# Router logits of a one-core attention and mixture-of-experts kernel: from transposes and a product on TensorE to products and row sums on VectorE

## The reference

```python
x = layernorm(x + attention(x))      # 16 heads of 16, rotated q and k, softmax over 2048 keys, then @ out_w + out_b
n = layer_norm(x, g1, be1)
y = x + n + (n @ mix_w + mix_b)
n2 = layer_norm(y, g2, be2)
probs = softmax(n2 @ router_w)       # router_w is 256 x 8: eight logits per token
topw, topi = top_k(probs, 2)         # each token goes to two of eight experts
out = y + sum over the two of topw * (silu(n2 @ w1[e] + b1[e]) @ w2[e] + b2[e])   # 256 -> 1024 -> 256
x = layernorm(out)
```

## Time and profile before

| | before |
|---|---|
| median of 3 runs | 1770.38 us |
| the profiled execution | 1769.97 us |
| its span, first to last instruction | 1768.3 us |
| mean granted TensorE clock | 0.966 of full speed |
| TensorE busy | 1646.8 us (93%) |
| ScalarE busy | 1234.6 us (70%) |
| VectorE busy | 534.5 us (30%) |
| GpSimd busy | 491.3 us (28%) |

### The profile page before, as it was taken

How to read it: one execution, slowest core, us unless ns; L and a number is a source line. 1 busy time by engine, 2 the same in 40 slices (tenths; PEclk the granted TensorE clock), 3 DMA queues, 4 the chain that set the end, 5 groups by cost and what they waited for, 6 DMA issues and landing times.

```text
span 1768.3 us, 46251 instructions
## 1 busy us (share of the span) xinstructions
PE 1646.8 (93%) x17948; PEld 934.9 (53%) x17949; DVE 534.5 (30%) x1421; ACT 1234.6 (70%) x1851; POOL 491.3 (28%) x512
## 2 busy tenths in 40 slices
PE   5986999998999999999999999998999999999991
PEld 3642333333333333333333333337899999999991
DVE  3441122633623623623623624634420000000004
ACT  2436899998997997997997997993344444444441
POOL 4750000121121121121121121123445444444441
PEclk9997999999999998999999999999999999999996
DMA  3567410011101153321101101165567766666645
GB/s 114 191 160 110 76 29 23 23 38 42 40 24 38 46 89 74 79 68 38 36 28 38 36 27 39 36 224 177 157 174 215 202 186 190 186 178 178 178 126 198
DMA packets 108822, 181.69 MB, mean 103 GB/s; under 512 B 14041, under 2 KB 80665, under 8 KB 108473
## 3 DMA queue, kind: packets, MB, share of 16 engines
q1 hardware_dynamic: 95346, 161.40, 31.4%
q0 software_dynamic: 13296, 17.77, 5.7%
HBM read 134.59 MB, written 40.18 MB: 99 GB/s over the span
## 4 chain that ended last, share of the span: by engine, by line
PE 77%; issue 4%; ACT 4%; another core or an unknown queue 3%; DVE 1%; DMA 1%; POOL 0%; SPq 0%; POOLq 0%; ACTq 0%; DVEq 0%
PE at_s L1241 23%; PE at_po L1253 22%; PE at_s L1364 14%; PE at_s L1377 13%; ACT place L1154 4%; PE at_small L1269 3%; PE at_small L1262 1%; PE at_po L1353 1%; DMA rows_out<-place,at_v 1%; DVE cb_ln_stats L578 1%; DVE place L1593 0%; POOL place L1097 0%; DMA place<-rows_out 0%; POOL place L1102 0%
## 5 line engine op out<-in xcount | busy, mean ns | idle before, releaser
L1154 ACT ACTIVATE place<-at_s 128x1024 f32<-128x1024 f32 x1024 | 957.9, 1142 | 92.3 <-PE at_s L1241 51.7
L1241 PE MATMUL at_s<-place 99*32 99x512 bf16 x8192 | 590.5, 388 | 35.1 <-ACT place L1154 24.9
L1253 PE MATMUL at_po<-place,at_v 128*32 128x512 f32 x4096 | 555.5, 602 | 9.4 <-issue 9.1
L1241 PEld LDWEIGHTS at_s<-place 99*32 99x32 bf16 x8192 | 202.7, 96 | 518.0 <-issue 250.2
L1364 PEld LDWEIGHTS at_s<-place 128*128 128x128 f32 x2272 | 265.7, 193 | 4.2 <-issue 0.8
L1364 PE MATMUL at_s<-place 128*128 128x128 f32 x2272 | 266.7, 276 | 0.0
L1171 ACT ACTIVATE place<-at_s,b_turned 128x128 f32<-128x128 f32 x568 | 161.8, 368 | 141.4 <-PE at_s L1364 139.5
L1377 PE MATMUL at_s<-place 128*128 x1136 | 256.9, 379 | 0.4 <-issue 0.4
L1377 PEld LDWEIGHTS at_s<-place 128*128 128x128 f32 x1136 | 210.4, 190 | 26.4 <-issue 0.7
L1253 PEld LDWEIGHTS at_po<-place,at_v 128*32 128x32 f32 x4096 | 132.6, 112 | 121.3 <-issue 23.1
L1016 POOL COPY at_v<-place 128x1024 f32<-128x1024 f32 x32 | 33.2, 1041 | 442.3 <-PE at_po L1253 431.7
(11 more groups left out here) (201 smaller groups left out, 971.7 us busy)
## 6 DMA issues: line engine op xcount, KB each, us to landing
place<-in_w SPq DMA_DIRECT2D x79, 1024.0 KB, 9.1
place<-k_parts SPq DMA_DIRECT2D x48, 256.0 KB, 9.3
place<-q_parts SPq DMA_DIRECT2D x192, 64.0 KB
at_v<-rows_in SPq DMA_DIRECT2D x71, 129.0 KB
x_in<-in_x SPq DMA_DIRECT2D x9, 512.0 KB, 4.8
q_parts<-qk_lower SPq DMA_DIRECT2D x16, 256.0 KB, 2.3
k_parts<-qk_lower SPq DMA_DIRECT2D x16, 256.0 KB, 2.5
at_heads_T<-at_o SPq DMA_DIRECT2D x128, 32.0 KB, 1.9
```

Source lines behind the costliest of these rows:

```text
L1154: nc.scalar.activation(probs[:, slot(n), :], p_s[n % BUFFERS][:, :], ACT.Exp).then_inc(exp_done, 1)
L1241: last = nc.tensor.matmul(p_s[n % BUFFERS][j:j + 32, s * 512:(s + 1) * 512], k_rows[0:ROWS_M, quad(q).start + h, kt * P + j:kt * P + j + 3 ...
L1253: last = nc.tensor.matmul(p_o[32 * h:32 * h + 32, :], v_one[q % 2][:, h, kt, :], probs[:, slot(q * NG + g), s * 512:(s + 1) * 512], start= ...
```

## The change

The router's logits are no longer computed by TensorE. `router_w` is loaded spread over all 128 partitions (each partition holds all 256 x 8 weights, 8 KB, by a broadcast load of 1 MB in place of one of 8 KB). For each of the four 128-token tiles of a group and each half of the experts VectorE multiplies the normalised row (256 columns, repeated four times) with the weights of four experts (read with a step of 8 elements, 32 bytes) into `weighted` (128 x 1024), and sums rows to four logits: 8 multiplications and 8 sums per group, each followed by a wait for its own completion. TensorE loses the second transposes and the router product, so a group has 7 jobs on `small`, not 10. The division is split off `copy_out` into `divide` and is placed later than the copy at three places; in unit 1 it stands between the ready signal of the first norm and the copy of the first transposes. The second `layer_norm`'s statistics now stand ahead of `copy_out(i + 1, 0)`, its application behind. TensorE's steps move: first transposes 48, 52 to 38, 40; mix product 56 to 62 to 44 to 50; counting 118 to 100; ScalarE's logit exponential 104 to 88. To make room, `den`, `passed` and the final norm's scratch now share memory with `turned`. In the last group's tail the points 17 to 19 go; the others keep their points.

```diff
 def layer_norm(dve, steps, out, inp, w):
     norm_scale(dve, steps, inp, w)
+    norm_apply(dve, steps, out, inp, w)
...
-    JOBS = 10
+    JOBS = 7
-    NORM_AT = {48: 0, 52: 1}
-    MIX_AT = {56: (0, 0), 58: (0, 2), 60: (1, 0), 62: (1, 2)}
-    SENT_AT = {80: 0, 84: 1}
-    ROUTER_AT = {88: 0, 90: 4}
-    COUNT_AT = 118
+    NORM_AT = {38: 0, 40: 1}
+    MIX_AT = {44: (0, 0), 46: (0, 2), 48: (1, 0), 50: (1, 2)}
+    COUNT_AT = 100
...
-        den = m.sb("at_den", [P, 512], F32)
-        router_w = m.sb("rt_router_w", [P, KC, E], F32)
+        router_w = m.sb("rt_router_w", [P, D, E], F32)
+        den = turned[:, 0, :]
...
-        STEPS = 3 * LN_STEPS + 19
+        STEPS = 3 * LN_STEPS + 19 + 4 * GT
-        TAIL_AT = {2: (14, 16), 3: (18, 20), 9: (48,), 10: (52,), 11: (56, 58), 12: (60, 62),
-                   17: (80,), 18: (84,), 19: (88, 90), 26: (118,)}
+        TAIL_AT = {2: (14, 16), 3: (18, 20), 9: (38,), 10: (40,), 11: (44, 46), 12: (48, 50),
+                   26: (100,)}
...
-                for dst, src in ((out_w, "out_w"), (mix_w, "mix_w"), (router_w, "router_w")):
+                for dst, src in ((out_w, "out_w"), (mix_w, "mix_w")):
                     sp.dma_start(dst[:, :, :], dram[src].rearrange("(s p) n -> p s n", p=P)).then_inc(loaded_w, 16)
+                sp.dma_start(router_w[:, :, :].rearrange("p d e -> p (d e)"),
+                             dram["router_w"].rearrange("d e -> (d e)").partition_broadcast(P)).then_inc(loaded_w, 16)
...
-                        if routed and n == 104:
+                        if routed and n == 88:
                             router(i - 1)
...
                     v.tensor_copy(o_sb[q % 2][:, :], p_o[:, :]).then_inc(o_copied, 1)
+
+                def divide(i, q):
+                    unit = i * UNITS + q
                     dve.wait_ge(o_copied, unit + 2)
...
                     layer_norm(v, steps, x1, x1, w)
+                    norm_scale(v, steps, x1, w)
                     if beside:
                         copy_out(i + 1, 0)
-                    layer_norm(v, steps, norm1, x1, w)
+                    norm_apply(v, steps, norm1, x1, w)
...
                                     ).then_inc(norm1_ready, 1)
-                    if not beside:
+                    if beside:
+                        divide(i + 1, 0)
+                    else:
...
                     dve.sem_inc(x2_ready, 1)
-                    if beside:
-                        copy_out(i + 1, 1)
-                    else:
+                    if not beside:
...
-                    turned_half(0)
-                    turned_half(1)
-                    job.arrived()
-                    logits = small[:, 0:GT * E].rearrange("p (a e) -> p a e", a=GT)
+                    dve.wait_ge(norm2_ready, i + 1)
+                    weighted = turned[:, :, :].rearrange("p k n -> p (k n)").rearrange("p (e d) -> p e d", e=E // 2)
+                    for a in range(GT):
+                        for some in (slice(0, E // 2), slice(E // 2, E)):
+                            steps.then(v.tensor_tensor(weighted, sent_rows[:, 0, a, 0:D].unsqueeze(1)
+                                                       .broadcast_to([P, E // 2, D]),
+                                                       router_w[:, :, some].rearrange("p d e -> p e d"), ALU.mult))
+                            steps.then(v.tensor_reduce(logit[:, a, some], weighted, AX.X, ALU.add))
+                        if a == 0 and beside:
+                            copy_out(i + 1, 1)
...
                     dve.sem_inc(shifted, 1)
-                    dve.sem_inc(small_read, 1)
                     if beside:
-                        copy_out(i + 1, 2)
+                        divide(i + 1, 1)
...
+                    if beside:
+                        copy_out(i + 1, 2)
                     job.arrived()
                     counts = small[:, 0:2 * GT * E].rearrange("p (n a e) -> p n a e", n=2, a=GT)
...
                     v.tensor_copy(pos[:, :, :], pos_f[:, :, :]).then_inc(placed, 1)
+                    if beside:
+                        divide(i + 1, 2)
```

More of the change, by code:

```diff
@@ L602, in layer_norm, with norm_apply @@
     norm_scale(dve, steps, inp, w)
+    norm_apply(dve, steps, out, inp, w)
+def norm_apply(dve, steps, out, inp, w):
     for a in range(GT):
@@ L764, in attend_route_experts @@
         final = room[:, at_quad:at_quad + NT * D].rearrange("p (a n) -> p a n", a=NT)
-        w_final = norm_scratch(m, "cb_ln", NT)
+        place_final = turned[:, 0, :]
+        w_final = {"stats": place_final[:, 0:NT * 6].rearrange("p (a n) -> p a n", n=6),
+                   "bits": place_final[:, NT * 6:NT * 7].bitcast(I32)}
+        w_final.update({n: place_final[:, NT * (7 + k):NT * (8 + k)]
+                        for k, n in enumerate(("var", "apart", "mean2", "rstd", "shift", "half", "t"))})
         loaded_sum = [m.sem(f"cb_loaded{g}") for g in range(PIECES)]
@@ L1308, in route @@
                         return product(mix_w, turned, (2 * half, 2 * half + 1), D, job, (first, first + 1))
-                    elif at in SENT_AT:
-                        pe.wait_ge(norm2_ready, i + 1)
-                        turn(sent_rows[:, 0, :, 0:D], SENT_AT[at], job)
-                    elif at in ROUTER_AT:
-                        first = ROUTER_AT[at]
-                        return product(router_w, turned, range(GT), E, job, range(first, first + 4))
                     elif at == COUNT_AT:
@@ L1565, in _ @@
                     copy_out(0, q)
+                    divide(0, q)
                 dve.wait_ge(loaded_w, 16 * 9)
@@ L1570, in _ @@
                     copy_out(i - 1, UNITS - 1)
+                    divide(i - 1, UNITS - 1)
                     route(i - 1, steps, job, True)
@@ L1575, in _ @@
                 copy_out(LAST - 1, UNITS - 1)
+                divide(LAST - 1, UNITS - 1)
                 making = Chain(dve, made)
@@ L1581, in _ @@
                 copy_out(LAST, UNITS - 1)
+                divide(LAST, UNITS - 1)
                 route(LAST, steps, job, False)
```

7 lines of the change are left out of this document (4 added, 3 removed).

## The result

The changed kernel takes 1857.97 us (median of four runs, 1852.97 to 1866.86) against 1771.52: a ratio of 1.0493, 95% interval 1.0472 to 1.0514. It is **slower by some 87 us**, where the prediction said 32 and a range up to 62. The direction was right, the size was not. All ratios leave out an execution that took over 1.5% longer than the fastest of its kernel; this concerns one of e5.

The account below looks back on a forecast made before the run. TensorE (93%) looks like the limit, but in the attention ScalarE's 32 exponentials a unit (29.4 us) are the floor. From 1770.38 us, −2.7 + 23 + 12.6 − 3 + 2 = +32 gives 1802; range 1744 to 1832.

Parts of the forecast that it names:

- main forecast: Whole kernel: the hole stays with the scatter and VectorE's lateness makes TensorE wait; +32 us, 1802 us, chance 0.47.
- hole: Units 3 and 0: ScalarE idle beside eight indirect DMAs, TensorE's clock at its lower level; together 52 us before.
- unit 1's transposes: First norm's second transposes, step 40: TensorE waits 2.7 us for VectorE's copy behind the division; with +0.6, seven times, +23.
- unit 1's copy: VectorE's p_o copy at unit 1's end, behind the second norm and first products: at about T + 39.7, done T + 40.4.
- The hole's term: Scatter moved to mid-unit 3: bounds −3 (49 of 52 us stay) or −52; −3 us taken.
- a lighter TensorE: Router work removed from TensorE: 0.4 us a group in unit 2, counted there; −2.7 us in the tail.
- I take 1.23, by the casts.: Router's strided multiplication on VectorE: 1.23 us each, between bounds 1.23 and 2.28; a tile of tokens 5.0.
- that rival: Router multiplications: strided reads slow, 2.3 us each, +5 us a group, 1837 us; chance 0.13.
- unit 0's copy: VectorE's p_o copy ending unit 0 (old time T), behind second norm's statistics: 1.8 us late, TensorE waits 1.05, +0.6.
- the step of unit 2: Head of unit 2: TensorE waits 2.2 us for unit 1's copy; unit 31.6 against 29.8, seven times, +12.6.
- Rival 1: Units 3 and 0: the hole goes once the scatter stands mid-unit; 1753 us, 1740 to 1765, chance 0.30.
- Rival 3: Units 1 and 2: VectorE's lateness absorbed by exponentials in hand; 1766 us, 1760 to 1772, chance 0.10.

Follow-up runs that it names:

- e5: Changed kernel with GpSimd waiting for each of the eight indirect DMAs to land: 1818.86 us, ratio 1.0593, on a chip where the kernel before took 1713.36.
- e15: Same edit as e5 (changed kernel, a wait after each indirect DMA) on a fourth chip: 1819.17 us, ratio 1.029 to the kernel before.
- e4: The paced kernel before: kernel before with GpSimd waiting after each indirect DMA until it has landed; 1717.66 us against 1773.19, ratio 0.969.
- e11: Same edit as e4 (kernel before, a wait after each indirect DMA) on a third chip: 1720.70 us, ratio 0.9705.
- e6: Changed kernel with weights read without a step, second transposes at 44, unit 1's copy ahead of the products, logits' exponential at 92, scatter paced: 1743.27 us.
- e1: Changed kernel with the router's weights stored expert by expert, so multiplications read them without a step: 1848.50 us, ratio 1.043 to the kernel before.
- e3: Changed kernel with unit 1's copy ahead of the first products, not behind them: 1873.04 us, ratio 1.057 to the kernel before.
- after: The changed kernel itself, against the kernel before: 1857.97 us, ratio 1.0493.
- e12: e6 with unit 0's copy inside the second norm's small chain, transposes at 40 and 46, mix product at 48 to 54: 1743.18 us.
- e13: Kernel before with GpSimd waiting after every second indirect DMA, on a fourth chip: 1719.62 us, ratio 0.9698 to the kernel before.
- e7: Same edit as e13 (kernel before, a wait after every second indirect DMA) on another chip: 1714.25 us, ratio 1.0001.

## Why the prediction missed

**What held.** The direction. The main forecast that the hole stays with the scatter and isn't tied to the change of group: shown by e15 and by ScalarE's gaps at 839.53 and 842.37. The price of the hole before, 52 us: e4 measures 55.5, e11 50. The place of both new waits, in unit 1's transposes (2.7 forecast, 3.02 measured) and at unit 1's copy. The row sum (1.15 to 1.25; 1.22). The hole's term, −0.4 a group: unit 3 is 2.0 longer, and unit 0, once the 2.6 us by which its copy is late are taken off (34.8 in e15 against 32.2 in e4), 2.3 shorter. That a lighter TensorE is worth next to nothing in the groups fits e6, whose units 2 and 3 together are no shorter than those of the paced kernel before, but isn't shown alone.

**The first step that failed: "I take 1.23, by the casts."** The strided multiplication takes 2.08 alone and 2.18 on average. The casts of 8 elements are 172 ns of mostly fixed time, and could not have shown a cost per element; by size, the nearest row was the upper end, 2.28 for 2048 elements. I had the rule that speaks against the change beside it (the Trainium skill, SBUF — State Buffer, § Door 1: The DMA port swizzle: each access that crosses to a new 16-byte line pays), and gave it 0.13. The trace agrees with the rule: 2183 ns with a step of 32 bytes, 1331 without (e1). But this step explains some 2 of the 8.1 us a group that are missing (12.8 measured, 4.7 forecast).

**But that rival, too, was priced short**, at 1837, though its sign, multiplications of 2 us, is what came, beside the main forecast's waits. Its own term is 1.4 us a group by e1's medians and 2.2 by units 1 and 2, not 5: the router's wait behind it did not come up, since the late copy gave it cover, as e3 shows. (The cover itself was added up wrongly: T + 36.5 − 1.8 + 2.2 + 22.9 is T + 59.8, not 59.) The size was missed by other terms, in us a group:

| term | forecast | measured |
|---|---|---|
| unit 0's copy, at VectorE | 1.8 late | 2.6 late |
| what it costs | TensorE waits 1.05, +0.6 | TensorE waits 1.8; ScalarE 1.26 in five groups, 2.55 in two |
| second transposes | TensorE waits 2.7, +2.7 | TensorE waits 3.0 in five groups, 1.6 in two; up to 3 more in three groups by the clock |
| unit 1's copy | TensorE waits 2.2 (4.3 with slow multiplications), +1.8 over before | TensorE waits 5.2, ScalarE 7.5 (4.95 and 6.7 in the group above) |
| hole | −0.4 | −0.3 |

**The largest miss is the step of unit 2, "TensorE waits 2.2"**: some 5.7 of the 8.1 us a group. It fails in two places.

First, the wait is more than twice as long. From unit 0's copy to unit 1's the prediction has 37.9 us (T + 1.8 to T + 39.7), and 41.6 were measured. Of the 3.7, `x2` is 0.8 (the statistics begin 24.6 behind the copy, not 23.7), the second norm up to its ready signal 0.8 (9.6, from 775.39 to 784.96, not 8.7), and the first two products 2.1 (7.5, where the prediction has 5.4 with GpSimd beside them). TensorE itself came 1.1 us later than forecast, so the wait grew by 2.7.

Second, I priced the wait at its own length and put the clock at nothing here; I had thought of it only for the transposes. The two copies of one group show what it does. Behind unit 0's, at full clock, ScalarE's next exponential starts 1.54 us after the weighing (751.67 to 753.21). Behind unit 1's, with the granted clock at 0.50, it starts 2.83 us after (793.28 to 796.11), and the next score is late once more, by 1.02. So the clock adds 1.3 + 1.0 = 2.3 us here, and 2.8 in the other groups, where the second gap is mostly 1.53. Some half a microsecond of each wait is absorbed by the exponentials in hand, as I had it for unit 0's copy: 1.8 of TensorE give 1.26 of ScalarE. In the two groups in which ScalarE lost 2.55 at unit 0's copy, the wait was the same 1.8 and the weighing behind it took 1.94 us.

That unit 0's copy came 2.6 late and not 1.8, and that the second norm took 0.8 more, has one origin: in each of the two a small instruction of VectorE took 0.97 in place of 0.16, at 748.25 and at 776.83, and ended with the GpSimd instruction beside it. It is so in all seven groups of after. The prediction had counted GpSimd only against the products.

**Rival 1** (the hole gone, 0.30) did not come; on the one chip without it the paced changed kernel was still 5.9% slower. **Rival 3** (absorbed) fell clearly.

**What stays open.** Why a chip shows the hole or doesn't: of the four chips of the experiments three showed it in every run of the kernel before, one in none of 19. By what path indirect DMAs hold up TensorE: in the trace it has nothing to wait for that the profile shows. Whether their number in flight or their rate does it. Why the clock fell behind some of the 1.8 and 3.0 us waits and not behind others of the same length. Why two of the seven groups of e6 are longer (unit 0 of the fourth is the longest of its kind in most profiles, those of the paced kernel before included), and e12's 5 to 7 us behind the attention. The division in its old place behind each copy, with new steps for all else, wasn't tried.

**What beats both kernels** is the kernel before with the scatter in pairs (e13) or singly (e4, e11): 1718 to 1721 us where the hole is, and for pairs no loss where it isn't (e7).

## What to carry to other kernels

A cost per element is bounded by rows of the same size, never by one in which the fixed part hides it; where a small and a large row disagree by a factor, take the large. When work is moved to an idle engine, write out that engine's program order with the start of each instruction, and carry a lateness through all that stands behind it: 30% busy says nothing about being on time. Price a wait of TensorE with the clock behind it: 5.2 us became 7.5 of ScalarE. A burst of indirect DMAs can stop other engines for microseconds; break it with waits before rearranging compute around the gap that it leaves.

## What was not expected of the hardware

**The hole**, 7 us a group of ScalarE time, follows eight indirect DMAs 1.27 us apart; it is gone with a wait after each, a seventh is left in the groups with a wait after each second, and a third of the time with a wait after each fourth. It was there on three of four chips.

**The clock behind a wait.** A wait of TensorE of some 5 us was followed by the lower level of the granted clock in all seven groups (0.50 over 793 to 796 us; weighings of 1.93 us for 1.07), one of 1.8 us in two of seven, one of 3.0 us in some.

**VectorE and GpSimd side by side.** In e6 the first product runs beside GpSimd's addition, VectorE's rows first, then GpSimd's:

```profile
1112.83 2.90 DVE L1524 TENSOR_TENSOR rt_turned<-rt_sent_rows,rt_router_w 128x1024 f32<-128x1024 f32 x1
...
1117.02 1.22 DVE L1524 TENSOR_TENSOR rt_turned<-rt_sent_rows,rt_router_w 128x1024 f32<-128x1024 f32 x1
```

```profile
1112.27 2.38 POOL L1051 TENSOR_TENSOR rt_sent_rows<-rt_norm,rt_be 128x1024 f32<-128x1024 f32 x1 [7.24 <-DVE rt_sent_rows L1513]
```

2.90 us against 1.22 for the same instruction: 1.7 lost to an addition of 2.38 that had started 0.56 earlier. In after VectorE started first and it was the addition that lost, 4.29 against 2.39, and then the second multiplication, 2.81 against 2.10. The row sum between them stayed at 1.22. Small instructions are struck too, 0.97 for 0.16 at 748.25 and 776.83. My 0.4 from the earlier trace rows, where GpSimd's instruction has one element, was too small by a factor of two for after (0.7) and of four for e6. This agrees with the rule of the Trainium skill (SBUF — State Buffer, § Who interferes with whom), an exclusive lock of the shared port pair for a whole instruction, which goes to the one that starts first, when VectorE's has two SBUF inputs and GpSimd's reads SBUF.
